# A graph stack on one core: the opening reordered (destination rows first, 128 by 25 counting, keys in two parts, norm product on POOL)

## What is computed

```python
h = relu(layernorm(x)); x = x + L0_gcn(h)        # degrees, norm_out, sum over edges, @ W, norm_in
h = relu(layernorm(x)); x = x + L1_attention(h)  # 8 heads, edge attributes, feed-forward
h = relu(layernorm(x)); x = x + L2_gat(h)        # gat with 3 heads, then with 1
h = relu(layernorm(x)); x = x + L3_sage(h)       # two mean aggregations
# inside L0_gcn, the part that the opening prepares:
deg_out = segment_sum(ones, src); norm_out = rsqrt(max(deg_out, 1))
agg = segment_sum((h * norm_out)[src], dst)      # the product @ W commutes with the sum
```

## Time and profile before

| | us |
|---|---|
| median of 3 runs | 3032.11 |
| lowest, highest | 3029.42, 3033.09 |
| the profiled execution, its time | 3027.89 |
| its span, first to last instruction | 3026.3 |
| PE busy | 2431.8 (80%) |
| DVE busy | 1378.1 (46%) |
| POOL busy | 1355.2 (45%) |
| ACT busy | 928.1 (31%) |

### The profile page before, as it was taken

One profiled execution on the slowest core, in us unless ns is written; L12 is line 12 of the kernel. 1 busy time (PEld: TensorE's weight loads), 2 busy tenths in 40 slices (PEclk: granted clock), 3 DMA queues, 4 the chain that ended last, 5 costly groups with the idle time before them and its releaser, 6 DMA issues.

```text
span 3026.3 us, 36316 instructions
## 1 busy us (share of the span) xinstructions
PE 2431.8 (80%) x12369; PEld 1811.7 (60%) x12369; DVE 1378.1 (46%) x3004; ACT 928.1 (31%) x1990; POOL 1355.2 (45%) x1419
## 2 busy tenths in 40 slices
PE   7799999748888886676888886675777777399998
PEld 7566666517777775454555553355777776266666
DVE  5855555447777775433444444232222222611313
ACT  4322222223333332453444443232222222300201
POOL 3000000177777773447777773327777775300000
PEclk7577778879888887667999999685555555699999
DMA  9447686049999994105777776204555554465360
GB/s 234 161 155 259 237 278 219 1 123 279 263 257 264 263 265 132 30 20 178 237 242 242 237 245 201 74 15 101 134 132 134 131 136 107 145 203 163 115 204 27
DMA packets 518577, 517.76 MB, mean 171 GB/s; under 512 B 154112, under 2 KB 463747, under 8 KB 517211
## 3 DMA queue, kind: packets, MB, share of 16 engines
q1 hardware_dynamic: 310333, 267.24, 29.4%
q0 software_dynamic: 50528, 115.22, 15.2%
q10 hardware_dynamic: 157534, 132.98, 14.0%
HBM read 301.13 MB, written 227.33 MB: 175 GB/s over the span
## 4 chain that ended last, share of the span: by engine, by line
PE 37%; POOL 30%; issue 12%; DVE 10%; DMA 7%; ACT 4%; SPq 1%; POOLq 0%; DVEq 0%; ACTq 0%
POOL arena L992 28%; PE ps L1496 10%; PE ps L1404 7%; PE ps L1414 6%; DMA arena<-t_attn,src_i 3%; DMA arena<-t_gat,src_i 2%; PE ps L1478 2%; PE ps L1569 2%; PE ps L1375 2%; DVE arena L2204 1%; PE ps L1693 1%; DVE arena L2142 1%; ACT arena L1023 1%; PE ps L1670 1%; PE ps L1602 1%
## 5 line engine op out<-in xcount | busy, mean ns | idle before, releaser
L1023 ACT ACTIVATE arena<-ps 128x544 f32<-128x544 f32 (+8 forms) x589 | 481.0, 826 | 1575.0 <-PE ps L1569 625.2
L992 POOL DMA_INDIRECT arena<-t_gat,src_i x784 | 740.7, 945 | 239.0 <-issue 233.5
L1569 PE MATMUL ps<-arena 128*128 128x136 f32 (+2 forms) x2352 | 650.5, 437 | 109.0 <-ACT arena L1023 58.2
L1569 PEld LDWEIGHTS ps<-arena 128*128 128x128 f32 x2352 | 447.4, 253 | 240.8 <-DVE arena L2204 91.6
L992 POOL DMA_INDIRECT arena<-t_attn,src_i x392 | 381.9, 974 | 119.5 <-issue 112.8
L1496 PE MATMUL ps<-arena 128*128 128x384 bf16 x1850 | 304.2, 328 | 36.6 <-DVE rec L2346 35.3
L1545 PEld LDWEIGHTS ps<-arena 128*128 128x128 f32 x1568 | 285.9, 266 | 35.3 <-issue 6.6
L2152 DVE TENSOR_TENSOR z_b<-arena,ps 128x12 f32<-128x12 f32 (+1 forms) x196 | 31.6, 161 | 559.6 <-DMA arena<-t_gat,src_i 503.1
L1496 PEld LDWEIGHTS ps<-arena 128*128 128x128 bf16 x1850 | 181.6, 98 | 159.0 <-issue 41.1
L1545 PE MATMUL ps<-arena 128*128 128x3 f32 (+1 forms) x1568 | 266.2, 292 | 5.8 <-ACT arena L1023 4.2
L955 POOL TENSOR_TENSOR arena<-arena,r_L_gnn_gamma 128x512 f32<-128x512 f32 (+1 forms) x7 | 8.1, 1150 | 543.0 <-ACT arena L1217 543.0
(11 more groups left out here) (325 smaller groups left out, 2973.3 us busy)
## 6 DMA issues: line engine op xcount, KB each, us to landing
ends_gat<-arena ACTq DMA_DIRECT2D x98, 774.0 KB, 4.1
arena<-adj_hbm SPq DMA_DIRECT2D x90, 640.0 KB, 3.9
same_b<-same_hbm SPq DMA_DIRECT2D x294, 128.0 KB
adj_hbm<-arena SPq DMA_DIRECT2D x9, 3200.0 KB, 11.2
ends_attn<-arena ACTq DMA_DIRECT2D x98, 272.0 KB, 4.7
ends_gat<-arena ACTq DMA_DIRECT2D x98, 258.0 KB, 3.8
arena<-edst SPq DMA_DIRECT2D x98, 256.0 KB, 4.3
starts_q<-zrow SPq DMA_DIRECT2D x28, 896.0 KB, 6.6
```

The lines of the kernel that those rows point to most:

```text
L992: g.indirect_dma_start(out=row_b[:, n % RB, k, 0:row_tab[p].shape[1]], out_offset=None, in_=row_tab[p], in_offset=bass.IndirectOffsetOnAxi ...
L1023: return a.activation(o, i, ACT.Copy)
L1569: i = mm(o, same_f[:, g % RB, k, :], msg[:, g % 4, k * W:(k + 1) * W], start=True, stop=True)
```

## The change

It does six things. (1) Only the 8 destination transfers count on `s_edge_r`; SP and ACT wait for them before they issue anything else, and ACT issues the three source transfers after that wait, on a semaphore of their own, for which DVE waits before its cast. (2) The count is 128 by 25: low 7 bits and high bits, so there is no join. (3) The keys of the first two chunks are made before the loop; those of the other eight inside it, one step in each of the batches 0 to 4, transposed and copied at batch 5. (4) The products `hn` and the first subtraction `r1` go to POOL, in batches 6 to 14 by ACT's order. (5) The equality matrices begin at batch 20 and are spread over the other 127; SP issues the weights ahead of them, and the zero fills earlier. (6) The first sparse product comes after batch 21 instead of 19, the next after 25, 29, 33.

```diff
+SAME0 = 20
+SOON = 2
+LATE_AT = 5
+def groups_by(b):
+    return max(0, b - SAME0) * NG // (NB - SAME0)
...
+            sp.wait_ge(s_edge_r, EDGE_R)                       # SP, after its 4 destination transfers
...
+            for o, i in weights:                               # SP, before its loop over the matrices
+                load(o, i)
...
-                if kept < NC - 1 and g == ((kept + 1) * PER + 3) * 2 // 3:
+                if kept < NC - 1 and g == groups_by((kept + 1) * PER + 3):
...
+            def by_node(j):                                    # POOL
+                if j == 0:
+                    pool.wait_ge(s_ln, ln_c.end)
+                    pool.wait_ge(s_out, out_c.end)
+                    pool.wait_ge(keys_ps, 4)
+                gt(tiles(hn, j), tiles(h_sb, j), norm..., ALU.mult).then_inc(pool_o.sem, 1)
+            def rest(j):
+                pool.wait_ge(act_o.sem, act_o.at("n0", "hi", j))
+                gt(tiles(hn, j), tiles(hn, j), split_of(j, 0), ALU.subtract).then_inc(pool_o.sem, 1)
+            in_turns(pool_o, "n0", hn=by_node, r1=rest)
...
+            act.wait_ge(s_edge_r, EDGE_R)                      # ACT
             act.dma_start(src_r[:, 0:3, :], ...).then_inc(s_src, 16)
...
+            keys_copied(0, SOON, 0, 1)
...
+                if b == LATE_AT:                               # ACT, in the loop
+                    keys_copied(SOON, NC, 4, 6)
+                for step, j in split_at(b):                    # batches 6 to 14
                     (hi if step == "hi" else mid)(j)
...
-                    i = mm(bank(7)[0:LOW, 0:2 * NT], hot_lo[:, slot, :, k], hot_hi[:, slot, :, k], ...)
+                    i = mm(bank(7)[:, 0:NT], hot_lo[:, slot, :, k], hot_hi[:, slot, :, k], ...)
-            pe.wait_ge(s_out, out_c.at("join"))
...
+            keys_of(0, SOON, 0, 1)                             # PE
...
-                if b >= PER and b % 4 == 3:
-                    spmm(b // PER - 1, b % PER // 4)
+                if b == LATE_AT:
+                    pe.wait_ge(step_keys, 2)
+                    keys_of(SOON, NC, 4, 6)
+                if b >= PER + 5 and b % 4 == 1:
+                    spmm((b - PER - 5) // PER, (b - PER - 5) % PER // 4)
...
+            dve.wait_ge(s_src, SRC_R)                          # DVE, before its cast
...
-                for o, parts, k in ((hot_lo, LOW, lo_f), (hot_hi, 2 * NT, hi_f)):
+                for o, parts, k in ((hot_lo, P, lo_f), (hot_hi, NT, hi_f)):
...
             dve.wait_ge(step_edges, 16 * 2 * NC)
+            for part_of in key_steps(0, SOON, key_math, step_keys):
+                part_of()
...
             for b in range(NB):
+                if b == SOON * PER:
+                    dve.wait_ge(keys_t, 4)
                 hot_steps(b)
+                if b in in_loop:        # 0-4 late keys, 5-6 spans, 8 to 16 seven times lowest
...
-                if b % 3 != 2:
-                    same(b // 3 * 2 + b % 3)
-                if b >= PER + 5 and b % 4 == 1:
+                for g in range(groups_by(b), groups_by(b + 1)):
+                    same(g)
+                if b >= PER + 7 and b % 4 == 3:
                     v_row(done)
```

More of the change, by code:

```diff
@@ L719, in _ @@
                 load_dst_row(g)
+            with nc.allow_non_contiguous_dma(reason="biases as columns"):
+                for o, i in weights:
+                    load(o, i)
             kept = 0
@@ L724, in _ @@
                     load_dst_row(g + UNROLL)
[L725 to L731, removed]
+                if g >= 10 and g % 2 == 0 and g // 2 - 5 < ZERO_PARTS:
+                    zeros(starts["attn"], ZERO_PARTS, g // 2 - 5, 256)
+                elif g in (71, 73):
+                    p = ("gat1", "gat2")[(g - 71) // 2]
                     zeros(starts[p], 1, 0, 392)
-                if kept < NC - 1 and g == ((kept + 1) * PER + 3) * 2 // 3:
+                if kept < NC - 1 and g == groups_by((kept + 1) * PER + 3):
                     store_adj(kept)
@@ L1903, in _, with key_steps, at, first @@
-            dve.wait_ge(key_math, 4)
-            stt(key_i[:, :, :].bitcast(F32), es[:, :, :].bitcast(F32), 512.0, key_i[:, :, :], ALU.mult, ALU.add)\
-                .then_inc(step_keys, 1)
+            v.tensor_copy(deg[:, 0, :], bank(7)[:, 0:NT]).then_inc(s_out, 1)
+            dve.wait_ge(s_out, out_c.at("max"))
+            ts(norm[:, 0, :], deg[:, 0, :], 1.0, None, ALU.max).then_inc(s_out, 1)
+            def key_steps(c0, c1, done, last):
+                def at(t):
+                    return t[:, c0:c1, :]
+                def first():
+                    ts(at(lo_s).bitcast(I32), at(es), P - 1, None, ALU.bitwise_and)
+                    ts(at(key_i), at(es), 7, 2, ALU.logical_shift_right, ALU.logical_shift_left).then_inc(done, 1)
+                def second():
+                    dve.wait_ge(done, 1)
+                    v.tensor_copy(at(lo_s), at(lo_s).bitcast(I32))
+                    ts(at(es), at(ed), DG - 1, None, ALU.bitwise_and).then_inc(done, 1)
+                def third():
+                    dve.wait_ge(done, 2)
+                    tt(at(key_i), at(key_i), at(es), ALU.bitwise_or)
+                    ts(at(ed), at(ed), 2, None, ALU.logical_shift_right).then_inc(done, 1)
+                def fourth():
+                    dve.wait_ge(done, 3)
+                    tt(at(es).bitcast(F32), at(ed),
+                       bc(step_f[:, 2, c0:c1].rearrange("p (c a) -> p c a", a=1), [P, c1 - c0, P]), ALU.not_equal).then_inc(done, 1)
+                def fifth():
+                    dve.wait_ge(done, 4)
+                    stt(at(key_i).bitcast(F32), at(es).bitcast(F32), 512.0, at(key_i), ALU.mult, ALU.add).then_inc(last, 1)
+                return first, second, third, fourth, fifth
```

151 lines of the change are left out of this document (63 added, 88 removed).

## The result

| us | before | changed |
|---|---|---|
| median of 11 runs each | 3027.67 | 3021.30 |
| lowest, highest | 3023.99, 3033.09 | 3013.38, 3029.74 |
| the profiled execution, its time | 3027.89 | 3018.48 |
| its span | 3026.3 | 3016.8 |

The ratio is 0.9979 with a 95% interval of 0.9971 to 0.9988: 6.4 us faster between the medians, where I had forecast 3.1 slower. Three of the experiments' kernels (the long pause, all keys ahead, the matrices from batch 0) were timed while the kernel before took 3600.18 us, so of them only stretches behind the count are compared.

What follows compares the result with a forecast made beforehand. PE was taken to bound the count and later loop, DVE the loop's opening; +1.2 - 13.2 - 10.5 + 16.8 + 8.8 = +3.1 us gave 3031.0 in the profiled execution, 3035.2 as median, range 3020 to 3050.

Steps and rivals of the forecast that it cites:

- The boundary, +8.8: At eight chunk boundaries PE idles about 1.1 us, waiting for ACT's first copy into a reused tile: 8.8 us slower.
- Rival (2): The chunk boundary costs nothing, as the copy is queued early: -8.8 us, 3026.4; chance .10.
- The start, +1.2: Before the count, the new load order shifts the last load, `attn_r`: 1.2 us later, bounds -3 to +4.
- The count, -13.2: The count with 128 by 25 pairs becomes bound by DVE and takes 34.2 us against 47.4: 13.2 us faster.
- Rival (4): The count's pair isn't faster: at 121 ns +13 us (3048), at 184 ns +38; chance .07.
- Count to loop, -10.5: Between count and first one-hot of the loop, keys of only two chunks: 4.2 us instead of 14.67, 10.5 faster.
- The loop's opening, +16.8: The loop's first 22 batches take 61.3 us instead of 44.5, POOL's time added to DVE's: 16.8 us slower.
- Rival (1): POOL and DVE overlap after all in the loop's opening: -9.7 us, 3025.5; chance .15.
- rival (3): POOL's gathers starve beside DVE's one-hots without pauses in the count, delaying the keys: +22 to 25 us, 3058; chance .09.

Runs made afterwards that it cites:

- the long pause: The changed kernel with ACT's first copy into a reused tile made three times over: 3611.26 us, ratio 1.0035 to the kernel before.
- two mirror edits: Sparse products one batch earlier in the changed kernel: 3019.61 us, ratio 0.9972; two batches later in the kernel before: 3029.22 us, ratio 1.0005.
- the split on DVE: The changed kernel with `hn` and `r1` back on DVE instead of POOL, all else as changed: 3016.30 us, ratio 0.9964 to the kernel before.

## Why the prediction was wrong, step by step

- **The boundary, +8.8: the step that failed.** Mechanism, place and length were right (1.07 us of idle PE against 1.1), the price was wrong. I took PE busy 40 of 40 us as "a microsecond of pause is one of time". The granted clock of 0.76 stood in that same row: PE was held back by its clock there, and a short pause came back as clock. The two mirror edits show it in both kernels: with the pause and without it a chunk takes 47.8, where the step had a chunk 1.1 longer. Rival (2) had the difference (5.7 faster than the median that it was reckoned from; measured 6.4) but for another reason, that there would be no pause.
- **The start, +1.2: mis-sized**, measured +6.2, beyond the bound of +4. Of this, 4.5 is `attn_r` landing at 32.85 instead of 28.32. I noted that x would be issued earlier and counted it as load on the transfers; with x in front, SP's issue of two pads took 7.31 us instead of .90, and one of 5.53 whose cause is open came on top. The destination rows landed at 7.6, not at 6.3. The other 1.7 I had at nothing: PE turns the 32 weight blocks in 6.15 us, where it took 4.45 before, at a granted clock of 1.00 both times. Why is open.

```profile
28.37 4.45 PE ps L1362 x32
```

- **The count, -13.2**: measured -12.9. A turn is 1.41; PE's pairs run at 64 to 71 ns (16 in 1.03, 24 in 1.71), near the 62 that I had taken. Rival (4) is out.
- **Count to loop, -10.5**: measured -10.1. As the run with all keys ahead showed, most of it was not a gain but a move.
- **The loop's opening, +16.8: mis-sized**, measured +11.9. The exclusion is there: without POOL's work DVE is busy for less with more to do. But I added POOL's 15.9 in full to DVE's work and then 4.9 of idle and 3.1 of PE behind it. The run with the split on DVE puts DVE's own work at 39.5 (I had 37.4) and what POOL added to it at 8.1; idle it was 8.4. So POOL did about half of its work while DVE waited, for `mid` above all, and I charged for both. Rival (1), no exclusion, is out: the rule of the Trainium skill ("SBUF — State Buffer", section "SBUF: two separate sides") that one of the two holds the port pair for its whole instruction fits a one-hot of 1.60 us where it takes .68 alone.
- **Starved gathers, rival (3)**: out. They slowed from one in 1.25 us to one in 1.41, a turn of DVE's, and ended before the count:

```profile
52.82 1.11 POOL L939 DMA_INDIRECT arena<-esrc,step_i  x1 [0.31 <-issue]
54.24 1.11 POOL L942 DMA_INDIRECT arena<-edst,step_i  x1 [0.30 <-issue]
```

With the boundary and the start mended the sum is 3.1 - 8.8 + 5.0 = -0.7, with the opening -5.6, with the two small differences (.3 and .4) the -4.9 of the marks. The start (5.0 too low) and the opening (4.9 too high) cancel by luck; that is why the sum misses by about the boundary's 8.8.

## What to carry to other kernels

Where PE is busy throughout and its granted clock is well under 1, ask of every pause or saving what the clock makes of it: here 1.07 us a chunk was free, 2.81 wasn't, and work taken out paid. Read it from the marks of several turns of the loop, not from one: they settle, and what an opening gains can be lost in part in the first of them (5.4 us at the first product, 3.0 at the loop's end). An idle engine that shares something with the busy one is no free place: `hn` and `r1` cost 7 us more on POOL than on DVE. And a large transfer that moves earlier on one queue can go with long issues on another. Where a queue stands idle in a wait, put there what the critical path waits for next: here twelve small loads, worth 10 us.

## What the runs showed of the hardware

A chunk's length didn't change with a pause of 1.07 us in two kernels (47.77, 47.76, 47.77, 47.80), and grew by 2.3 for one of 2.81. Eleven kernels with the same matmuls and a pause of 0 or 1.07 settle at 47.74 to 47.85 from the third chunk on, and with a fifth of the sparse products' matmuls left out at 44.33 to 44.40. Beside two-input operations of POOL a DVE one-hot took up to 1.63 us instead of .68. POOL's indirect transfers fall into step with DVE's operations when these leave no gap, one to a turn of 1.41 us, and are not starved by them. An issue on SP took 7.31 us for two transfers while ACT issued x for 8.78 (5.71 to 8.91 in seven other kernels with that order), and .90 with x moved behind it; with twelve small loads put ahead of the lists on SP it took 1.04, and x's own issue 3.86.
